# First expert's rows of an attention + mixture-of-experts kernel: ten batch rows gathered from HBM, six selected on chip by one-hot products

## The reference, cut to what matters

```python
x = x + xattn(layernorm(x), ctx)              # x: 16 x 128 x 256, 2048 tokens of 256 numbers
x = x + ffn(layernorm(x))

def ffn(hidden, combine_weights, top_idx, W1, b1, W2, b2):
    x = hidden.reshape(-1, 256)
    tok = top_idx.T                           # 8 experts, 512 tokens for each, with repeats
    gathered = x[tok]
    h = gelu(einsum('ecd,edf->ecf', gathered, W1) + b1[:, None, :])      # f = 1024
    out_e = einsum('ecf,efd->ecd', h, W2) + b2[:, None, :]
    weighted = out_e * combine_weights[tok, e_ids][..., None]
    return zeros.at[tok.reshape(-1)].add(weighted)
```

## Time and profile before

| what | us |
|---|---|
| median of 3 runs | 297.89 (297.28 to 299.18) |
| the profiled execution's own time | 297.96 |
| its span, first to last instruction | 296.2 |
| PE busy in the span | 264.8 (89%) |
| DVE, ACT, POOL busy | 228.5, 176.5, 158.9 |

### The profile page before, as it was taken

How to read it: one execution, slowest core, us unless ns; L and a number is a source line. 1 busy time by engine, 2 the same in 40 slices (tenths; PEclk the granted TensorE clock), 3 DMA queues, 4 the chain that set the end, 5 groups by cost and what they waited for, 6 DMA issues and landing times.

```text
span 296.2 us, 5382 instructions
## 1 busy us (share of the span) xinstructions
PE 264.8 (89%) x1677; PEld 234.0 (79%) x1677; DVE 228.5 (77%) x534; ACT 176.5 (60%) x338; POOL 158.9 (54%) x150
## 2 busy tenths in 40 slices
PE   6559999998826999999999999999999999999960
PEld 2449879896722798999999898999999999989960
DVE  3698999999881499797797787797887887966341
ACT  2437699786633667648557666657566666745410
POOL 3446845566456741466566565646645645416605
PEclk9999999999985999999999999999999999999976
DMA  6995237454352674544644543554445441201201
GB/s 206 208 364 144 71 107 212 142 161 138 114 184 82 216 256 139 144 138 158 196 137 126 176 173 124 160 163 164 143 133 197 144 140 48 71 2 63 63 11 64
DMA packets 29137, 42.06 MB, mean 142 GB/s; under 512 B 5249, under 2 KB 22859, under 8 KB 28992
## 3 DMA queue, kind: packets, MB, share of 16 engines
q1 hardware_dynamic: 24512, 29.61, 32.6%
q0 software_dynamic: 4608, 12.24, 13.1%
HBM read 33.93 MB, written 8.45 MB: 143 GB/s over the span
## 4 chain that ended last, share of the span: by engine, by line
PE 70%; DVE 8%; issue 8%; POOL 5%; DMA 4%; ACT 2%; DVEq 0%; ACTq 0%; POOLq 0%
PE bank L1060 18%; PE bank L1061 18%; PE bank L1062 18%; PE bank L1132 4%; PE bank L1101 3%; POOL out_dram L507 2%; PE bank L1147 2%; POOL x_all L501 1%; PE bank L1168 1%; PE bank L1172 1%; PE bank L1169 1%; DVE hn_cnat L721 1%; PE bank L1121 1%; DVE setup_or_probs L816 1%; DMA x_all<-token_rows,idx_all 1%
## 5 line engine op out<-in xcount | busy, mean ns | idle before, releaser
L663 ACT ACTIVATE keysT<-bank,biasT 128x512 f32<-128x512 f32 (+1 forms) x65 | 43.9, 675 | 65.2 <-PE bank L1062 56.1
L507 POOL DMA_INDIRECT out_dram<-h,sidx x32 | 38.4, 1200 | 46.6 <-DVE h L950 39.3
L501 POOL DMA_INDIRECT x_all<-out_dram,idx_all x32 | 38.7, 1211 | 23.8 <-DMA out_dram<-h,sidx 16.2
L1060 PE MATMUL bank<-x_hi,w_hi 128*128 128x512 f32 (+1 forms) x114 | 45.2, 396 | 0.0
L1061 PE MATMUL bank<-x_lo,w_hi 128*128 128x512 f32 (+1 forms) x114 | 44.5, 390 | 0.0
L1062 PE MATMUL bank<-x_hi,w_lo 128*128 128x512 f32 (+1 forms) x114 | 44.0, 386 | 0.0
L497 POOL DMA_INDIRECT x_all<-token_rows,idx_all x28 | 27.4, 980 | 22.1 <-DVE factor L1006 15.4
L958 DVE SCALAR_TENSOR_TENSOR junk<-idx_rows,idx_f,normed 128x512 bf16<-128x512 bf16 (+1 forms) x32 | 38.9, 1215 | 0.0
L989 DVE TENSOR_TENSOR w_lo<-w_raw,w_hi 128x512 fp32r<-128x512 f32 x56 | 38.3, 684 | 0.1
L1062 PE MATMUL bank<-w_hi,g_lo 128*128 128x256 f32 x128 | 36.2, 283 | 0.0
L1060 PE MATMUL bank<-w_hi,g_hi 128*128 128x256 f32 x128 | 36.1, 282 | 0.1
(11 more groups left out here) (141 smaller groups left out, 711.9 us busy)
## 6 DMA issues: line engine op xcount, KB each, us to landing
w_raw<-in_L_ffn_W_dram SPq DMA_DIRECT2D x32, 512.0 KB, 3.7
hn_cnat<-in_ctx_dram SPq DMA_DIRECT2D x8, 256.0 KB, 2.7
idx_rows<-in_L_ffn_top_idx_dram SPq DMA_DIRECT2D x8, 256.0 KB, 4.0
out_dram<-x SPq DMA_DIRECT2D x8, 256.0 KB, 2.4
token_rows<-xn SPq DMA_DIRECT2D x7, 256.0 KB, 2.2
x_all<-in_x_dram SPq DMA_DIRECT2D x2, 768.0 KB, 11.2
hn_cnat<-in_L_ffn_b_dram SPq DMA_DIRECT2D x1, 1024.0 KB, 6.7
x_all<-in_x_dram SPq DMA_DIRECT2D x2, 256.0 KB, 3.7
```

The costliest lines, as they stand in the source:

```text
L501: g.indirect_dma_start(accg[:, t, :], None, flat, list_of(e, t)).then_inc(acc_in, 16)
L507: g.indirect_dma_start(flat, idx(sidx[:, t:t + 1].bitcast(U32), 0), newrow[:, t, :], None, bounds_check=N - 1, oob_is_err=False).then_inc( ...
L663: a.activation(g32[:, f % NG, c], ps_up[j % 2][:, c], ACT.Gelu_apprx_tanh, bias=bias)
L1060: t_.matmul(dst, lhs_hi, rhs_hi, start=first, stop=False)
```

## The change

Expert 0's 512 rows come in two parts. The rows that belong to pairs 0 to 4 are gathered from `token_rows` in pair 6, two tiles before and two behind POOL's `rstd`. The places of pairs 5 to 7 in `token_rows` are written with zeros at the start of the program (two DMAs of 768 pieces of 512 bytes, behind the first two parts of the token lists), so a slot whose token is in a late pair gathers zeros. SP waits for the four gathers before it stores pair 5. The late rows never go through HBM for expert 0. POOL makes six one-hot matrices (128 tokens of a batch row by 512 slots, `is_equal` of the token list with the token's number), four in pair 5 and two in pair 7. PE multiplies the high and the low parts of the late rows with them and adds both to the same two banks into which it also brings the gathered rows. The high parts are made on ACT, the low ones on POOL (pair 5) and DVE (pairs 6 and 7).

Besides that: expert 0 runs in whole steps like the others. The `keep_warm` calls behind the last pair are gone. The lists of tokens are loaded two parts in each of pairs 0 to 2 instead of one part in each of pairs 0 to 5. The low parts of weight pieces 6 and 7 go to DVE, behind `x_lo`. The two `last_rstd` of POOL stand ahead of the fill of `seen` instead of behind it, the last pair's shift of pair 6 stands ahead of the first half's x2, and ACT loads its gelu table inside pair 7.

```diff
+    EARLY_PAIRS = NPAIR - 3
+    EARLY = 2 * EARLY_PAIRS
...
+        onehot = w_hi[:, 1, 0:(NB - EARLY) * C].rearrange("p (b c) -> p b c", c=C)
+        late_hi = [M_hi[:, :, :], gateT_hi[:, :, :], hnT_hi[:, 0, :, :]]
+        late_lo = [M_lo[:, :, :], gateT_lo[:, :, :], hnT_lo[:, 0, :, :]]
...
-        ps_pv_last = [banks[7][:, 0:H], banks[2][:, 0:H]]
+        ps_pv_last = [banks[7][:, 0:H], banks[4][:, 0:H]]
...
+            sp.wait_ge(ident_rdy, 2)
+            zeros = causal[:, S:2 * S].rearrange("p (b c) -> p b c", b=1).broadcast_to([P, NB - EARLY, S])
+            for j in range(KH):
+                sp.dma_start(rows_v[:, EARLY:NB, j * S:(j + 1) * S], zeros).then_inc(zeros_in, 16)
...
+                if r == EARLY_PAIRS:
+                    for t in range(NT):
+                        sp.wait_ge(first_rows_in[t], 16)
...
-                if r + 2 < IDX_PARTS:
-                    load_lists(r + 2)
-                if r == NPAIR - 1:
-                    for t in range(NT):
-                        sp.wait_ge(first_rows_in[t], 16)
+                if 2 * r + 3 < IDX_PARTS:
+                    load_lists(2 * r + 2)
+                    load_lists(2 * r + 3)
...
+            def one_hot(b):
+
+                g.tensor_scalar(onehot[:, b - EARLY, :].rearrange("p (t q) -> p t q", t=NT), first_list,
+                                tok_f[:, b - EARLY:b - EARLY + 1], None, ALU.is_equal).then_inc(onehot_rdy, 1)
+
+            def first_late_low():
+
+                pool.wait_ge(late_hi_rdy, 1)
+                pool.wait_ge(xn_rdy, 2 * EARLY_PAIRS + 2)
+                g.tensor_tensor(late_lo[0], xn2[:, EARLY_PAIRS % 2, :, :], late_hi[0].bitcast(F32), ALU.subtract)\
+                    .then_inc(late_lo_rdy, 1)
+
+            def gather_first_rows(tiles):
+
+                pool.wait_ge(comb_in, 16)
+                pool.wait_ge(idx_in, 16)
+                pool.wait_ge(zeros_in, 16 * KH)
+                for s in range(2):
+                    pool.wait_ge(xn_out[s], 16 + 16 * ((EARLY_PAIRS + 1 - s) // 2))
+                for t in tiles:
+                    g.indirect_dma_start(xg[:, 0, t, :], None, rows_dram, list_of(0, t)).then_inc(first_rows_in[t], 16)
...
+                if isinstance(p, int) and p == EARLY_PAIRS:
+                    pool.wait_ge(idxrows_in, 16 * IDX_PARTS)
+                    pool.wait_ge(tok_rdy, 2)
+                    for b in range(EARLY, EARLY + 4):
+                        one_hot(b)
+                if isinstance(p, int) and p == EARLY_PAIRS + 1:
+                    gather_first_rows(range(NT // 2))
...
+                if isinstance(p, int) and p == EARLY_PAIRS + 1:
+                    gather_first_rows(range(NT // 2, NT))
+                if is_last(p):
+                    for b in range(EARLY + 4, NB):
+                        one_hot(b)
+                elif not (isinstance(p, int) and p == LAST - 1):
                     expert0_lo(p)
+
...
+                    expert0_hi(p)
+                    act.wait_ge(setup_mm, 4)
+                    a.copy(biasT[:, :], banks[0][:, 0:NE * NF]).then_inc(setup_ev, 1)
...
+                    a.activation(table_junk[:, :], junk[:, 0:2], ACT.Gelu_apprx_tanh)
...
+                if isinstance(p, int) and p > EARLY_PAIRS:
+                    late_high(p - 1, 1 - s)
...
+            def late_high(p, s):
+
+                act.wait_ge(xn_rdy, 2 * p + 2)
+                a.copy(late_hi[p - EARLY_PAIRS], xn2[:, s, :, :]).then_inc(late_hi_rdy, 1)
...
-            normalised_x2(LAST, 1, 3)
-            expert0_hi(NPAIR - 1)
-            act.wait_ge(setup_mm, 4)
-            a.copy(biasT[:, :], banks[0][:, 0:NE * NF]).then_inc(setup_ev, 1)
+            act.wait_ge(xn_out[1], 16 * 3 + 16)
+            act.wait_ge(late_lo_rdy, 1)
+            act.wait_ge(shift_rdy, NPAIR)
+            a.activation(xn2[:, 1, 0, :], x2[:, 1, 0, :], ACT.Identity, bias=shift2[:, 1, 0:1], scale=rstd2[:, 1, 0:1])\
+                .then_inc(last_xn[0], 1)
+            for b in range(2):
+                act.wait_ge(shift_rdy, NPAIR + b)
+                a.activation(late_hi[2][:, b, :], x2[:, 1, b, :], ACT.Identity, bias=shift2[:, 1, b:b + 1],
+                             scale=rstd2[:, 1, b:b + 1]).then_inc(late_hi_rdy, 1)
 
...
+            dve.wait_ge(late_hi_rdy, 2)
+            v.tensor_tensor(late_lo[1], xn2[:, 1 - last_s, :, :], late_hi[1].bitcast(F32), ALU.subtract)\
+                .then_inc(late_lo_rdy, 1)
...
+            dve.wait_ge(shift_rdy, NPAIR + 1)
+            dve.wait_ge(xn_out[last_s], 16 * (NPAIR // 2))
+            v.tensor_scalar(xn2[:, last_s, 1, :], x2[:, last_s, 1, :], rstd2[:, last_s, 1:2], shift2[:, last_s, 1:2],
+                            ALU.mult, ALU.add).then_inc(last_xn[1], 1)
+            for b in range(2):
+                dve.wait_ge(late_hi_rdy, 3 + b)
+                dve.wait_ge(last_xn[b], 1)
+                v.tensor_tensor(late_lo[2][:, b, :], xn2[:, last_s, b, :], late_hi[2][:, b, :].bitcast(F32),
+                                ALU.subtract).then_inc(late_lo_rdy, 1)
...
+            x_lo_part(0, 0)
+            dve.wait_ge(whi_rdy, NPAIR)
+            dve.wait_ge(wlo0_rdy, NPAIR - 2)
+            for piece in range(NPAIR - 2, NPAIR):
+                col = slice(piece * PIECE, (piece + 1) * PIECE)
+                v.tensor_tensor(w_lo[:, 0, col], w_raw[:, col], w_hi[:, 0, col].bitcast(F32), ALU.subtract)\
+                    .then_inc(wlo0_rdy, 1)
...
+                    pe.wait_ge(log_rdy, 2 * NPAIR)
+                    pe.wait_ge(late_hi_rdy, 1)
+                    late_rows(0, 0, late_hi, True)
...
+            def late_rows(n, b, part, first=False, last_one=False):
+
+                pe.wait_ge(onehot_rdy, 2 * n + b + 1)
+                for k in range(KH):
+                    last = t_.matmul(ps_xT[k][:, :], part[n][:, b, k * P:(k + 1) * P], onehot[:, 2 * n + b, :],
+                                     start=first, stop=last_one)
+                    if last_one:
+                        last.then_inc(xT_mm, 1)
+
             each_pair(pe, attention)
-            pe.wait_ge(bias_in, 16)
-            t_.transpose(banks[0][:, 0:NE * NF], bias_rows[:, :], ident[0:NE * NF, 0:NE * NF]).then_inc(setup_mm, 1)
+            for t in range(NT):
+                pe.wait_ge(first_rows_in[t], 16)
+                for k in range(KH):
+                    t_.matmul(ps_xT[k][:, t * P:(t + 1) * P], xg[:, 0, t, k * P:(k + 1) * P], ident[:, :],
+                              start=False, stop=False)
+            pe.wait_ge(late_lo_rdy, 1)
+            for b in range(2):
+                late_rows(0, b, late_lo)
+            pe.wait_ge(late_hi_rdy, 2)
+            for b in range(2):
+                late_rows(1, b, late_hi)
+            pe.wait_ge(late_hi_rdy, 3)
+            late_rows(2, 0, late_hi)
+            pe.wait_ge(late_lo_rdy, 2)
+            for b in range(2):
+                late_rows(1, b, late_lo)
+            pe.wait_ge(late_hi_rdy, 4)
+            late_rows(2, 1, late_hi)
+            for b in range(2):
+                pe.wait_ge(late_lo_rdy, 3 + b)
+                late_rows(2, b, late_lo, last_one=b == 1)
 
             def rows_transposed(e, s, rounds):
...
-            for s in range(2):
-                pe.wait_ge(xn_out[s], 16 * (NPAIR // 2) + 16 + 16 * s)
-            keep_warm(8)
-
-
-            for t in range(NT):
-                pe.wait_ge(first_rows_in[t], 16)
-                half, col = t // (NT // 2), t % (NT // 2) * P
-                for k in range(KH):
-                    last = t_.transpose(ps_xT0[half][k][:, col:col + P], xg[:, 0, t, k * P:(k + 1) * P], ident[:, :])
-                    if t % (NT // 2) == NT // 2 - 1:
-                        last.then_inc(xT_mm, 1)
-                if t % 2 == 0:
-                    keep_warm(2 - t // 2)
-                if t == NT // 2 - 1:
-                    up(0, 0, 0)
-                    up(0, 0, 1)
-
             def expert(e, s, use):
-                if is_first(e):
-                    down(e, s, 0)
...
```

194 lines of the change are left out of this document (85 added, 109 removed).

## The result

The kernel after takes **305.13 us** (median of 4, 304.72 to 305.92), the kernel before 297.76 (297.28 to 299.18) on the same chip: ratio 1.0246, 95% interval 1.021 to 1.0282. The change makes the kernel slower by 7.4 us; 296.5 us were forecast. The profiled execution took 305.37 us, span 303.6, PE clock 0.97. In every ratio, executions that took over 1.5% longer than the fastest of the same kernel are left out. Measured once more (chip D, experiment 11), before took 298.37 and after 304.01: 1.0182 (1.0105 to 1.0259). On chip C the comparison stays open, which experiment 8 comes to.

The account below looks back on a forecast made before the run. PE, busy from 103.1 us, was taken as the bound, with the chain of waits up to `x_hi` ahead of it. 7.0 + 0.7 - 2.0 - 1.4 - 2.1 - 0.5 - 0.2 = 1.5 us off 297.96: 296.5, range 291.5 to 301.5.

Parts of the forecast that it names:

- The one-hots in pair 5: Four one-hots on POOL ahead of pair 5's `rstd`, taken at 1.1 us each: 2.0 us lost.
- what is removed: Wait chain from the last `rstd` to expert 0's `x_hi`: it starts at 90.05 instead of 97.06, 7.0 us gained.
- pair 7's body: Pair 7 ahead of its `rstd`: POOL's subtraction for pair 5 (1.26 us) fits there, no loss counted for it.
- The rule on POOL's reads: One-hots' strided list reads on POOL: an estimated half longer, 1.65 us each, making the sum about zero.
- rival B: One-hots on POOL take 2 us each, 3.7 us lost in all, 301.7 us; chance 0.15.
- Held instructions: DVE instructions with two SBUF inputs take turns with POOL's 512-column reads; L708 and its twin wait one one-hot each.
- Pair 7's one-hots: Two one-hots behind pair 7's `rstd` hold two of DVE's mixing instructions for one one-hot each: 2.1 us lost.
- Pair 6: Gathers delay `rstd` by 0.9 us and DVE's L786 is held behind them: 1.4 us lost in all.
- the forecast's 0.2 for the clock: PE's clock falls late in the hole behind the last pair, hitting a few matmuls: 0.2 us lost, between 0 and 2.
- The start of the program: Zero writes ahead of pair 2's context load on the same queue: 0.5 us lost, between 0 and 2.5.
- Expert 0, and expert 1's rows: Expert 0 in whole steps gains 0.7 us; expert 1's gathers end near 102, PE wants the rows near 105.
- rival C's second half: PE waits for expert 1's rows; with its first half, delayed context, gain 0 to -1.5, 298.5 us; rival's chance 0.10.

Follow-up runs that it names:

- experiment 11: Before unchanged, after unchanged, and before with the second biases' load held until expert 0's fifth gelu, all on chip D: 298.24, 304.01 and 298.91 us.
- experiment 8: Before and after, both unchanged, on chip C: before 306.21 us, after 307.77, 308.05, 308.91 and once 301.94.
- experiment 1: A separate small kernel running only one-hots of 128x512 in several forms: strided 1995 ns, packed 1566 ns on POOL, 0.66 us on DVE.
- experiment 4: After with each one-hot cut to 8 of its 512 columns, late rows coming out as zeros: 299.14 us, ratio 1.0017 to before.
- tuned kernel: After with all the change's work kept but placed anew, one-hots mostly one by one: 298.68 us on chip C (0.9769 to before), 297.53 on D (0.9968).
- experiment 5: After with expert 1's gathers ahead of the fill of `seen`, on chip B: 303.59 us.
- experiments 2 and 3: 2: before with only the zero writes added, 300.08 us (1.0037 to before). 3: after with the zero writes moved to pair 3, 304.37 us (1.0192 to before).
- experiment 6: After with all six one-hots on DVE, three in pair 5 and three in pair 6, on chip B: 303.58 us.

## Why the prediction was wrong

**The step that failed: "The one-hots in pair 5 ... I take 1.1".** The bounds 0.62 and 1.26 came from rows of other operations, and the value from a select with 128 columns. A one-hot takes 2.15 us in the kernel, 2.00 alone (experiment 1). "Against: 1.26 is the longest row of this width" treated a two-input operation as a ceiling for a one-input one, which the 1.57 us packed form contradicts. With 2 us the prediction's own working gave 5.3 for pair 5; 4.27 was measured, because the first one-hot does not wait for the residual sum as I had it (65.3, 5.78 us behind pair 4's `rstd`): it starts right behind the product L431, at 66.69, 4.44 behind. Experiment 4 shows what the length is worth: 6 to 7 us between 2.15 and 0.5 us. At the 1.1 that I had taken the kernel would by the estimate there still have missed 296.5 by 2.5 to 5 us. So two more steps failed with this one, each with a size of its own below: the 7.0 for what is removed (4.54 measured) and pair 7's body, which I had put at nothing (2.31).

**The rule on POOL's reads.** The Trainium skill, GPSIMD Engine Reference, "Performance pitfalls for Q7 kernels", has an element at 2.9 instead of 1.9 cycles where the step is over 8 bytes, which I made half more. This case's row says 27% more for the whole instruction (1995 against 1566 ns), and that need not differ from the page, which speaks of the cost of an element: with 8 columns a one-hot still takes 0.50 us (experiment 4), and an estimate with that taken off both is 40% more. The direction was right and spoke for rival B; my base under it was what was off. "The sum about zero" at 1.65 us didn't fit rival B's own slope either: from 1.35 on, 0.4 to 0.6 for each 0.1 makes it 1.2 to 1.8 lost.

**Held instructions.** That two-input DVE work and POOL's work take turns is right, the list of victims was not: L748 and L752 were not held (0.15 and 0.17), the residual sum was, and so in part were L843 and L770 (0.45 and 1.09, with short one-hots 0.17 and 0.73). Pair 7's one-hots: 2.1 lost by forecast, 1.85 measured, which is near by luck. Not two operations were held for a one-hot each: L927 took 0.9 more and the second L922 0.3 more (0.77), and the second row's shift waited 0.72 for a `rstd` behind the one-hots, a wait that the prediction didn't have.

**Pair 6 and pair 7's body.** 1.4 lost was forecast for the gathers and the held residual sum; 1.02 and 2.31 came. I had put the mixing free and the subtraction for pair 5 at nothing. The mixing L821 was held to 2.69 us, through POOL's sum (87.39 to 88.68) and subtraction (88.63 to 89.92) in a row. In the tuned kernel, where the subtraction stands elsewhere and a one-hot is in the pair, the mixing still took 2.50, beside a gather's issue and the sum, which began 0.65 us behind it; but pair 7 takes 8.18 us (86.76 - 78.58) instead of 9.11. So some 0.9 of the 2.31 goes with the subtraction's place, as far as nothing else that was moved counts, and the rest stays.

**What is removed.** 7.0 gained was forecast, 4.54 came. Of the difference of 2.5, L964 is 1.3 (1.67 us for the 0.4 of the sum; 0.41 in experiment 5, without the memset beside it), the last `rstd` 0.4, the two subtractions 0.3, and the late matmuls, at a clock of 0.50 in 102 to 104, the rest; the forecast's 0.2 for the clock, with near 1.00 ahead of `x_hi`, was low as well. I had noted that the fill of `seen` moves behind `last_rstd` and not asked who runs beside it then.

**The start of the program.** 0.5 forecast, bound 2.5; PE waits 2.34 and pair 4 is 2.73 late, yet experiments 2 and 3 put the whole at 1.1 (0.1 to 2.1) and at some 1 to 2 us of the kernel's time. The bound was right and the value low.

**Expert 0, and expert 1's rows.** 0.7 was forecast from `x_hi` on; 0.99 was lost instead: 1.47 for the wait before expert 1's transposes, less 0.48. "POOL is through `seen` near 97, its four gathers near 102, and PE wants the rows near 105" left 3 us between the last issue and the need. In the trace the margin was 3.8 (the last gather's issue ends at 110.6, PE wanted the rows at 114.45), so the order held; but that gather took 6.29 us to land, for the 3.01 of the first gather before, and the DMA share was 0.98 to 1.06 in 110 to 116 us. The landing was the missing term. This is rival C's second half; experiment 5 gives back 1.2 of it and of L964 together.

**Rival B** had the mechanism and a price of 301.7. What it lacks to the profiled 305.4 is 2.5 in the removal, 2.0 at the start, 1.7 at experts 0 and 1 and 0.2 in pair 7, less 1.0 in pair 5, 0.4 for the gathers and 1.2 at the end. The small 0.2 is luck: its 4.0 for pair 7's one-hots were 1.85, and 2.31 came from the mixing that it had free.

**Left open.** What ScalarE waits for at expert 0 on chip C (and, by its 306 us, perhaps on B), in the kernel before alone. On the first chip and on D after is 2.5 and 1.8% slower; on C it isn't decided. The explanation above rests on traces of after, whose pair 5 is the same on the first chip, C and D: 13.01, 12.95 and 12.97 us. The 0.3 to 0.4 us by which pair 5 is longer than before even with short one-hots (9.05 against 8.74) isn't explained.

## What to carry to other kernels

An operation that no row of the trace shows has no ceiling from rows of other operations, so where the sum hangs on it let the range follow its length. Added work on an engine with free time is free only in pieces shorter than a gap and out of the way of the other engine's two-input instructions: the same one-hots cost 6 to 7 us in a lump, 0.7 to 0.9 each in the wrong part of a gap, and next to nothing right behind the residual sum. When a wait is shortened, ask what was hidden in it, here the fill of `seen` and expert 1's gathers.

## What the hardware showed that I had not expected

- A POOL instruction with one packed 512-column input and a column operand takes 1.57 us, one with two such inputs 1.26.
- A DVE instruction with two SBUF inputs was held through a row of two-input POOL operations without a gap: the mixing took 2.69 us beside two, 3.09 beside the same two in experiment 6 and 2.50 beside a gather's issue and the sum in the tuned kernel, and ended 0.56 or 0.57 us behind the last of them each time. Beside one-input one-hots it was not: L828 ended at 68.86, when the first of four in a row was done. A memset on POOL held a DVE instruction with one SBUF input and two column operands (1.67 for 0.41).
- DVE's own one-hots, with one SBUF input, doubled from 0.61 to 1.3 us beside POOL's two-input work.
- The kernel before took 298 us on the chip of the first comparison, A and D, and 306 on B and C, in 19 runs or more on each of the four; its trace on C has a wait of 5.24 us that no kept trace of a kernel derived from after shows.
